# Expert rows gated at their eviction and added in memory by the indirect store, partly filled blocks first

## What is computed

```python
logits = xf @ Wg                                  # xf: normalized rows, 2048 x 256
top_w, top_i = jax.lax.top_k(logits, 2)
top_w = jax.nn.softmax(top_w, axis=-1)
combine = jnp.einsum('nk,nke->ne', top_w, jax.nn.one_hot(top_i, 8, dtype=xf.dtype))
h = jnp.einsum('nc,ech->enh', xf, W1)             # W1, W2: 8 x 256 x 512
g = jnp.einsum('nc,ech->enh', xf, W2)
y = jnp.einsum('enh,ehc->enc', jax.nn.silu(h) * g, W3)
out = jnp.einsum('enc,ne->nc', y, combine)        # and h_residual + out is returned
```

## Time and profile before

| what | value |
|---|---|
| time, median of 3 runs | 590.05 us (589.65 to 590.31) |
| the profiled execution: its time / its span | 591.61 us / 589.9 us |
| PE, DVE, ACT, POOL busy | 74%, 52%, 33%, 20% of the span |
| chain that ended last | PE 59%, DVE 26%, issue 5%, DMA 4%, ACT 4% |
| bytes moved by DMA | 45.08 MB, mean 76 GB/s |

### The profile page before, as it was taken

How to read it: one execution, slowest core, us unless ns; L and a number is a source line. 1 busy time by engine, 2 the same in 40 slices (tenths; PEclk the granted TensorE clock), 3 DMA queues, 4 the chain that set the end, 5 groups by cost and what they waited for, 6 DMA issues and landing times.

```text
span 589.9 us, 8973 instructions
## 1 busy us (share of the span) xinstructions
PE 437.5 (74%) x3202; PEld 283.0 (48%) x3203; DVE 308.0 (52%) x836; ACT 192.5 (33%) x360; POOL 120.4 (20%) x132
## 2 busy tenths in 40 slices
PE   0689797796666545327461999999999999999920
PEld 0345444454554434315361556666656565656520
DVE  0695676765988895899967166162101010101018
ACT  1234445255455312024221332433332323333210
POOL 5111010100110011020102153233232323233210
PEclk9979998989959757757655899999999999999985
DMA  9997010190170003400110011211111111111149
GB/s 173 248 194 144 0 39 2 34 290 4 44 282 18 24 1 105 182 0 17 40 51 19 18 46 44 72 37 45 46 50 40 44 44 47 42 53 36 36 139 306
DMA packets 36579, 45.08 MB, mean 76 GB/s; under 512 B 5504, under 2 KB 29824, under 8 KB 36416
## 3 DMA queue, kind: packets, MB, share of 16 engines
q1 hardware_dynamic: 30608, 34.10, 21.2%
q0 software_dynamic: 3744, 10.23, 5.3%
q10 hardware_dynamic: 2192, 0.27, 0.5%
HBM read 33.05 MB, written 9.31 MB: 72 GB/s over the span
## 4 chain that ended last, share of the span: by engine, by line
PE 59%; DVE 26%; issue 5%; DMA 4%; ACT 4%; POOL 1%; SPq 0%; DVEq 0%; POOLq 0%; ACTq 0%
PE psum L1696 23%; PE psum L1713 11%; PE psum L1433 8%; PE psum L1446 3%; PE psum L1704 3%; DMA M3s<-in_x_dram 2%; PE psum L1471 2%; PE psum L1686 2%; DMA M2s<-mixture_rows_out 1%; PE psum L1458 1%; DVE st_att L864 1%; PE psum L1505 1%; DVE mx L898 1%; DVE st_in L864 1%; DVE H L954 1%
## 5 line engine op out<-in xcount | busy, mean ns | idle before, releaser
L1358 DVE TENSOR_TENSOR QT<-QT,psum 128x512 f32<-128x512 f32 x39 | 26.8, 688 | 182.5 <-PE psum L1696 182.5
L1696 PE MATMUL psum<-M1s,KT 128*128 x156 | 75.9, 610 | 1.3 <-issue 1.2
L1433 PE MATMUL psum<-M2s,M1s 128*128 128x512 f32 x128 | 61.0, 633 | 19.6 <-DVE M2s L744 19.6
L1713 PE MATMUL psum<-M3s,KT 128*128 x312 | 74.2, 381 | 1.5 <-ACT KT L673 0.8
L1696 PE MATMUL psum<-M2s,KT 128*128 x156 | 73.4, 593 | 0.0
L448 POOL DMA_INDIRECT mixture_rows_out<-O,dst_i x39 | 39.2, 1005 | 153.8 <-ACT O L679 150.3
L1713 PEld LDWEIGHTS psum<-M3s,KT 128*128 128x128 f32 x312 | 58.7, 190 | 23.4 <-issue 17.4
L679 ACT ACTIVATE O<-psum 128x256 f32<-128x256 f32 x39 | 15.0, 384 | 114.6 <-PE psum L1713 114.6
L1433 PEld LDWEIGHTS psum<-M2s,M1s 128*128 128x128 f32 x128 | 25.3, 203 | 48.9 <-issue 29.4
L1696 PEld LDWEIGHTS psum<-M2s,KT 128*128 128x128 f32 x156 | 29.9, 192 | 37.9 <-issue 37.9
L437 POOL DMA_INDIRECT KT<-mixture_rows_in,src_i x39 | 40.0, 1025 | 35.3 <-DVE src_i L1318 23.9
(11 more groups left out here) (328 smaller groups left out, 688.6 us busy)
## 6 DMA issues: line engine op xcount, KB each, us to landing
M3s<-in_x_dram SPq DMA_DIRECT2D x4, 1024.0 KB, 11.1
M3s<-in_L_ffn_W_dram SPq DMA_DIRECT2D x1, 4096.0 KB, 15.4
M2s<-in_L_ffn_W_dram SPq DMA_DIRECT2D x1, 4096.0 KB, 15.9
M1s<-in_L_ffn_W_dram SPq DMA_DIRECT2D x1, 4096.0 KB, 14.2
M3s<-in_x_dram SPq DMA_DIRECT2D x4, 992.0 KB, 15.2
M1s<-vtok SPq DMA_DIRECT2D x64, 34.0 KB, 1.9
M1s<-mixture_rows_out SPq DMA_DIRECT2D x4, 512.0 KB, 7.4
M2s<-mixture_rows_out SPq DMA_DIRECT2D x4, 512.0 KB, 8.3
```

Of the source, the lines that this page charges most:

```text
L1358: v.tensor_tensor(sil[:, u, :], sil[:, u, :], bank[3], ALU.mult).then_inc(v_gated, 1)
L1433: last = mm(bank[6 + c], W1s[:, r, P * c:P * (c + 1)], xr[:, i % 2, r].rearrange("p b l -> p (b l)"), start=(n == 0), stop=(n == STRIDE - 1))
L1696: last = mm(z, xrT[:, u, c, :], w[:, bass.ds(e, 1), c, :].rearrange("p a h -> p (a h)"), start=(c == 0), stop=(c == CH - 1))
L1713: last = mm(bank[6][:, 0:DM], actT[:, u, c, :], M3s[:, bass.ds(e, 1), c, :].rearrange("p a d -> p (a d)"), start=(c == 0), stop=(c == HC - 1))
```

## The change

- H is stored to memory too, step by step, into `acc` (still named `mixture_rows_out`, now 2048 rows and 128 spare ones, which get zeros). SP issues each store behind the one of the normalized rows.
- Each slot's rows are multiplied by their gates at ACT's eviction (scale = a column of gate_slot), and POOL's indirect store adds them to the token's row (compute_op = add). One token has rows in two slots, so each store waits until the one before has landed (d_deliver). yrow has four buffers instead of two.
- The gates must be known before slot 0's eviction and, for the other 22 slots, before slot 17's. gates_of makes them and splits each into three bf16 parts, gate_tables puts them into the 0/1 tables, and PE turns these into columns per slot (gate_columns: 24 matmuls of 51 columns between slot_rows(0) and slot_rows(1), 32 of 66 columns in step 15). slot_gates adds the three parts. The exp for the gates moves ahead of slot 0 and into step 9.
- In the last 22 slots the partly filled block of each expert comes first (move_last, wrap_slots): slots 17 to 24 hold them, slots 25 to 38 hold whole blocks. When store 24 has landed, SP copies `acc` to the output in memory, and the stores of slots 25 to 38 add to the output itself. MIXED is 25.
- POOL has fetch(j+3) then deliver(j) in iteration j up to j = 24, no store in iteration 25, then deliver(j-1). The pieces of routing in steps 9 to 12 move to steps 9 to 16. ACT's loop over the last slots is written out. The tail (loads, gates, updates, stores) is gone.

```diff
     REST = SLOTS - FULL
+    WHOLE = REST - E
+    MIXED = FULL + E
     FAR = float(P * 1024)
...
-    ys = nc.dram_tensor("mixture_rows_out", [2 * NTOK + SLOTS * P, DM], F32, kind="Internal").ap()
-    out_rows = out.rearrange("b l d -> (b l) d").rearrange("(t p) d -> p t d", p=P)
+    acc = nc.dram_tensor("mixture_rows_out", [NTOK + P, DM], F32, kind="Internal").ap()
+    out_rows = out.rearrange("b l d -> (b l) d")
     xs_tiles = xs.rearrange("(t p) d -> p t d", p=P)
-    ys_tiles = ys[0:2 * NTOK, :].rearrange("(k t p) d -> p k t d", p=P, k=2)
+    acc_tiles = acc[0:NTOK, :].rearrange("(t p) d -> p t d", p=P)
...
-        yrow = part(O, 0, 2 * DM).rearrange("p (u d) -> p u d", u=2)
-        back = [part(m, 0, TILES * DM).rearrange("p (t d) -> p t d", t=TILES) for m in (M1s, M2s)]
+        yrow = part(O, 0, 4 * DM).rearrange("p (u d) -> p u d", u=4)
+        zeros = part(EO, 0, DM)
+        gate_table = [part(m, 0, 3 * t * n).bitcast(BF16).rearrange("p (k t m a) -> p k t m a", k=2, t=t, m=3)
+                      for m, t, n in ((PT, FIRST, FULL), (vtok, TILES, REST))]
...
+            sp.wait_ge(g_const, 20)
+            sp.dma_start(acc[NTOK:NTOK + P, :], zeros).then_inc(d_zero, 16)
...
+                sp.wait_ge(v_ssm_added, i + 1)
+                sp.dma_start(acc_tiles[:, TS * i:TS * (i + 1), :], H[:, TS * i:TS * (i + 1), :]).then_inc(d_acc[i], 16)
+            sp.wait_ge(d_deliver, 16 * MIXED)
+            sp.dma_start(out_rows.rearrange("(p r) d -> p (r d)", p=P),
+                         acc[0:NTOK, :].rearrange("(p r) d -> p (r d)", p=P)).then_inc(d_copied, 16)
+            sp.wait_ge(d_copied, 16)
+            sp.wait_ge(d_deliver, 16 * SLOTS)
...
             def deliver(j):
                 if j == 0:
+                    for i in range(last):
+                        pool.wait_ge(d_acc[i], 16)
+                    to = acc[0:FIRST * P, :]
+                elif j < FULL:
+                    to = acc[0:FIRST * P, :]
+                elif j < MIXED:
+                    to = acc
+                else:
+                    to = out_rows
+                if j == FULL:
+                    pool.wait_ge(d_acc[last], 16)
+                    pool.wait_ge(d_zero, 16)
                     pool.wait_ge(v_dst, 1)
-                if j == FULL:
-                    pool.wait_ge(v_dst, 2)
+                if j == MIXED:
+                    pool.wait_ge(d_copied, 16)
                 pool.wait_ge(a_slot_out, j + 1)
-                gp.indirect_dma_start(ys, bass.IndirectOffsetOnAxis(ap=dst_i[:, j:j + 1], axis=0),
-                                      yrow[:, j % 2, :], None).then_inc((d_deliver0, d_deliver1)[j % 2], 16)
+                wait(pool, d_deliver, 16 * j)
+                gp.indirect_dma_start(to, bass.IndirectOffsetOnAxis(ap=(src_i if j < FULL else dst_i)[:, j:j + 1], axis=0),
+                                      yrow[:, j % 4, :], None, compute_op=ALU.add).then_inc(d_deliver, 16)
...
-                deliver(j)
+                if j < MIXED:
+                    deliver(j)
+                elif j > MIXED:
+                    deliver(j - 1)
+            deliver(SLOTS - 1)
...
+            def gap_exp(n, ts):
+                act.wait_ge(v_logit_gap, n)
+                a.activation(rs[:, 4, ts], rs[:, 3, ts], ACT.Exp).then_inc(a_pair_gate, 1)
+            gap_exp(2, slice(0, FIRST))
...
+            def slot_out(j):
                 act.wait_ge(p_down, j + 1)
-                if stored is not None:
-                    act.wait_ge((d_deliver0, d_deliver1)[u], stored)
-                a.activation(yrow[:, u, :], bank[6][:, 0:DM], ACT.Copy).then_inc(a_slot_out, 1)
...
+                if j == 0:
+                    act.wait_ge(v_gate_slot, 1)
+                if j == FULL:
+                    act.wait_ge(v_gate_slot, 2)
+                wait(act, d_deliver, 16 * (j - 3))
+                a.activation(yrow[:, j % 4, :], bank[6][:, 0:DM], ACT.Copy, scale=gate_slot[:, j:j + 1]
+                             ).then_inc(a_slot_out, 1)
...
+                if j == 9:
+                    gap_exp(3, slice(FIRST, TILES))
+                if j == 11:
+                    table_rows(1)
+                slot_out(j)
...
+            def move_last(n):
+                ln(v.tensor_tensor(ra[:, 2, 0:n], ra[:, 7, 0:n], eb(W_lim, n), ALU.is_gt))
+                own()
+                ln(v.tensor_tensor(ra[:, 3, 0:n], ra[:, 2, 0:n], eb(last_at, n), ALU.mult))
+                own()
+                ln(v.tensor_tensor(ra[:, 4, 0:n], ra[:, 4, 0:n], ra[:, 3, 0:n], ALU.add))
+                own()
+            def pair_slots(n):
                 ln(v.tensor_tensor(ra[:, 5:7, 0:n], ra[:, 0:2, 0:n], ra[:, 4:5, 0:n].to_broadcast([P, 2, n, E]), ALU.mult))
...
+            def wrap_slots():
+                ln(v.tensor_scalar(far_slot[:], slot_in, float(REST), -float(REST), ALU.is_equal, ALU.mult))
+                own()
...
+            def rest_targets(z, lo, n):
+                f = [src_f[:, k, lo:lo + n] for k in range(3)]
+                for k, (s, w) in enumerate(((0, E), (E, n - E))):
+                    ln(v.tensor_scalar(f[2][:, s:s + w], z[:, s:s + w], 0.5, unread[:, k:k + 1], ALU.is_lt, ALU.mult))
+                own()
+                v.tensor_tensor(dst_i[:, lo:lo + n], f[2], f[1], ALU.add).then_inc(v_dst, 1)
+            def gates_of(n, ts):
+                dve.wait_ge(a_pair_gate, n)
+                ln(v.tensor_scalar(rs[:, 7, ts], rs[:, 4, ts], 1.0, None, ALU.add))
+                own()
+                ln(v.reciprocal(gates[:, 0, ts], rs[:, 7, ts]))
+                own()
+                ln(v.tensor_tensor(gates[:, 1, ts], gates[:, 0, ts], rs[:, 4, ts], ALU.mult))
+                own()
+                ln(v.tensor_copy(gate_part[:, 0, :, ts], gates[:, :, ts]))
+                own()
+                ln(v.tensor_tensor(gate_rest[:, :, ts], gates[:, :, ts], gate_part[:, 0, :, ts], ALU.subtract))
+                own()
+                ln(v.tensor_copy(gate_part[:, 1, :, ts], gate_rest[:, :, ts]))
+                own()
+                ln(v.tensor_tensor(gate_part[:, 2, :, ts], gate_rest[:, :, ts], gate_part[:, 1, :, ts], ALU.subtract))
+                own()
+            def gate_tables(which, tiles, n):
+                dve.wait_ge(d_xs[(1, STEPS - 1)[which]], 16)
+                for m in range(3):
+                    r = v.tensor_tensor(gate_table[which][:, :, :, m, :], in_slot[which],
+                                        kt(gate_part[:, m, :, 0:tiles], n), ALU.mult)
+                r.then_inc(v_gate_table, 1)
+            def slot_gates(which, lo, n, z):
+                dve.wait_ge(p_gate_table, which + 1)
+                g = gate_slot[:, lo:lo + n]
+                ln(v.tensor_copy(g, z[:, 0:n]))
+                own()
+                ln(v.tensor_tensor(g, g, z[:, n:2 * n], ALU.add))
+                own()
+                v.tensor_tensor(g, g, z[:, 2 * n:3 * n], ALU.add).then_inc(v_gate_slot, 1)
...
-            slot_experts(0, FULL, F_end)
+            first_experts()
             dve.wait_ge(p_table, 1)
-            token_rows(bank[7], 0, FULL, None)
+            token_of(bank[7], 0, FULL)
+            gates_of(1, slice(0, FIRST))
+            gate_tables(0, FIRST, FULL)
             expert_added(3, bank[4])
+            slot_gates(0, 0, FULL, bank[1])
...
+                if j == 10:
                     positions(TILES, ALU.is_le, R_lim, R_at)
-                if j == 10:
-                    slots_hot(1, TILES, REST)
+                    move_last(TILES)
+                    pair_slots(TILES)
+                    wrap_slots()
+                if j == 11:
+                    slots_hot(1, TILES, REST, far_slot)
                     table_tiles(1, TILES, REST)
                     rows_of(FIRST, TS)
                     rows_hot(3)
-                if j == 11:
-                    slot_experts(FULL, REST, R_end)
                 if j == 12:
+                    rest_experts()
+                    gates_of(2, slice(FIRST, TILES))
+                if j == 13:
                     dve.wait_ge(p_table, 2)
-                    token_rows(bank[1], FULL, REST, unread[:, FULL:SLOTS])
+                    token_of(bank[1], FULL, REST)
+                    rest_targets(bank[1], FULL, REST)
+                if j == 14:
+                    gate_tables(1, TILES, REST)
+                if j == 16:
+                    slot_gates(1, FULL, REST, bank[7])
...
-                dve.wait_ge(d_back[i], 32)
-                for n in range(TS * i, TS * (i + 1)):
-                    ln(v.scalar_tensor_tensor(H[:, n, :], back[0][:, n, :], rs[:, 8, n:n + 1], H[:, n, :],
-                                              ALU.mult, ALU.add))
-                own()
-                for n in range(TS * i, TS * (i + 1)):
-                    v.scalar_tensor_tensor(H[:, n, :], back[1][:, n, :], rs[:, 9, n:n + 1], H[:, n, :],
-                                           ALU.mult, ALU.add).then_inc(v_final, 1)
...
```

(12 more changed lines are left out.)

154 lines of the change are left out of this document (71 added, 83 removed).

## The result

| | before | after |
|---|---|---|
| time, median of 6 runs | 589.86 us (588.58 to 592.56) | 584.64 us (583.22 to 586.43) |
| ratio, 95% interval | | 0.990 (0.987 to 0.993) |
| profiled execution: time / span | 591.61 / 589.9 us | 584.18 / 582.0 us |
| PE, POOL busy | 74%, 20% of the span | 76%, 25% of the span |

What follows compares the result with a forecast made beforehand. TensorE was taken to bound 340 to 567 us, then a 23 us tail with DMA engines 84% busy. 570.4 + 0.6 + 0.2 + 1.6 = 572.8 us of span, plus 0.15: 573.0; forecast 570.3 to 576, full range to 584.

Steps and rivals of the forecast that it cites:

- Term 1: Program's end: tail goes, last two stores form a series, span ends 0.6 us after landing, at 570.4 (569.1 to 574.2).
- X: An adding store's time from issue to landing: taken as 3.3 us, between 2.4 and 5.2.
- Term 2: GpSimd's queue in the slots: cost 0 while X + 0.3 stays under 5.8 us; fetch needed two slots later.
- Term 3: Copy of accumulator to output between slots 24 and 25: TensorE stalls X + D − 12.7, 0.6 us (0 to 6.7).
- D: Time of the accumulator's copy to the output: taken as 10 us, between 8.1 and 14.2.
- Term 4: Before slot 0: earlier fetch, gate building and 1.1 us of gate matmuls; cost 0.2 us (−0.3 to 0.6).
- Term 5: Inside the slots: second gate table's matmuls cost 1.6 us (1.3 to 2.2); DVE's longest slot and table loads covered.
- The adding stores set the pace: Rival for the slots: if X + 0.3 exceeds 5.8 us, each slot costs X + 0.3, slower; chance 0.09.

Runs made afterwards that it cites:

- drop_last: The changed kernel without the call that stores block 38, SyncE waiting for 38 stores: 579.66 us, ratio 0.982 to the kernel before.
- before_no_tail: The kernel before without the tail's loads, updates on VectorE and its wait, H stored to the output during the slots: 574.08 us, ratio 0.971.
- late_drain: fetch_first with GpSimd itself waiting until all 39 stores have landed before its program ends: 579.69 us, ratio 0.980 to the kernel before.
- fetch_first: The changed kernel with GpSimd asking for block j+3 ahead of storing block j-1 in every iteration: 577.34 us, ratio 0.977 to the kernel before.

## Why the prediction was wrong, by its steps

- **Term 1, "the span ends 0.6 later": the step that failed at the end.** The 0.6 us were taken from an end at which the last thing to finish was a plain store of SyncE. With GpSimd's store last, its DRAIN was 4.3 us behind the landing: 3.9 us too few (drop_last, before_no_tail, late_drain). The row was in the trace before, from 565.9 to 573.5, and the prediction did not ask what the tail was hiding. 569.1, my lower end of this term, could not be reached by any X.
- **Term 1, X: mis-sized.** Forecast 3.3, measured 3.8, inside its bounds; no run shows that both sources of a row are read side by side, for which 3.3 was taken. Store 38 was delayed by the series to 573.82, some 1.4 us behind its rows; forecast 0.4. X alone made 0.5 of that. The pause on POOL between a landing and the next store is 0.8 us (569.21 + 3.85 to 573.82) and not 0.30, another 0.5.
- **The sum of Term 1.** From the last eviction to the end 9.9 us (572.13 to 582.0), forecast 4.6 (565.84 to 570.4).
- **Term 2, "needed two slots later" and "Cost 0": the step that failed in the slots.** It looked at whether POOL's queue keeps pace, which it does (X + 0.3 < 5.8), and not at when the fetch behind the store goes out. The fetch of block j+3 comes behind store j−1, and its rows are wanted about one slot behind that store's eviction. The store's issue, which I left at 1.0 us, takes 1.6 and up to 3.6. So the lead shrank by 0.6 us and more. The slots grew by 8.05 us (227.07 to 235.12) where Terms 3 and 5 forecast 2.2, 5.9 too few; with the fetch ahead of the store in both kernels they grow by 2.5, so 5.5 of it is this step (fetch_first gave 7.5 back, 2.0 of which the kernel before had lost too).
- **Term 3, the copy: right in kind, wrong in its terms' sizes.** D was 8.3 us (forecast 10, lower bound 8.1), X + D 12.1 instead of 13.3. By the prediction's formula that leaves 0.6 us of cover, which the store's longer issue, 0.6 us, uses up. Yet slot 28 took 0.65 us more: the fetch landed at 507.17 + 2.7 = 509.9, 0.2 us ahead of its transposes, and the gap "issue" came ahead of the next up matmuls. That 0.6 was forecast is luck, errors of both signs. The page's rate from the Trainium skill ("DMA: Bandwidth & Descriptors", section "Latency and other measured facts") would have made D 11.5 by the prediction's estimate; this copy was faster, and the measurement decides.
- **Term 4: right as far as it can be read.** The gate matmuls stand at 321.0 to 322.1, 1.1 us as forecast. The profile after runs 2.0 us ahead by 300 us already, ahead of this term's work; eviction 0 is 1.76 ahead, so 0.2 us were lost between, as forecast. That run-to-run difference hides 2 us of the miss in the spans.
- **Term 5: right.** Slot 15 took 1.56 us more (forecast 1.6), seen in fetch_first without the fetch's share. The terms of DVE's longest slot add up to 4.3 us and not to the 4.0 that stands there, but slot 10 took 5.83 us, so it was covered. The table load cost nothing that a slot shows. Not foreseen was what DVE's long operations do to POOL's issues.
- **The sum in spans.** 582.0 − 572.8 = 9.2: 5.9 in the slots, 5.3 at the end, less 2.0 of the run's earlier start. The times miss by 11.6, not 9.2, because the last step, 0.15 us from a span to the median, joined the span of one execution (591.61 us, 1.7 above its span) to the median of others; after, the median is 2.6 above the profiled span. These 2.5 us are mostly the same earlier start.
- **The rivals.** "The adding stores set the pace" named the right suspect with the wrong lever: it is not X + 0.3 against 5.8, but the issue in front of a fetch.

The Trainium skill, "Collectives: The Full Stack", section "The bandwidth ceiling", puts the price of an add, in the ring steps of a ReduceScatter, at its second source read. The trace agrees in kind: the queue has twice the packets for the same bytes. But X grew by 1.4 us, not by the 0.5 that the prediction worked out from the rate; for these rows of 1 KB the bytes alone do not give the price.

## What to carry to other kernels

Before you take a tail away, look at what each engine still does under it, the end of its own program too; GpSimd pays there for the DMAs that it gave, and a drain placed where it idles moves that payment. A DMA issue that gets longer is to be costed at what stands behind it in its engine's queue, by the lead that is left, and not by whether the queue keeps pace. Order a queue so that what others wait for soonest goes first.
